# Idle places and shapes on TensorE in a decoder kernel's local attention: fillers, spreads and transposes moved or cut in halves

## The reference

```python
def attn_layer(x, Wqkv, qs, ksc, Wo):
    q, k, v = split(x @ Wqkv)                   # 16 heads of 64
    q, k = l2norm(q) * qs, l2norm(k) * ksc
    q = q * cos * scale + rotate_half(q) * sin * scale
    k = k * cos / scale + rotate_half(k) * sin / scale
    sim = q @ k (this window of 32 and the one before) * 8, masked
    out = softmax(sim) @ v
    return out @ Wo
def ffn_layer(x, g, bln, W1, b1, W2, b2):
    xn = (x - mu) / jnp.sqrt(var + 1e-05) * g + bln
    a, gate = jnp.split(xn @ W1 + b1, 2, -1)
    return a * gelu(gate) @ W2 + b2
for i in range(6):
    x = attn_layer(shift_tokens(x), ...) + x
    x = ffn_layer(shift_tokens(x), ...) + x
```

## Time and profile before

| | us |
|---|---|
| median of 3 runs | 1740.59 (1736.71 to 1741.67) |
| the profiled execution | 1734.79 |
| its span | 1732.9 |
| PE busy | 1564.7 |
| DVE busy | 1155.8 |
| ACT busy | 928.1 |
| POOL busy | 589.0 |

### The profile page before, as it was taken

The page is one execution under the profiler, slowest core; times in us unless marked ns, Lnnn a source line. Parts: engine busy times, 40 slices in busy tenths (PEclk is TensorE's granted clock), DMA queues, the critical chain, the costliest instruction groups (busy, mean ns, idle before and its releaser), DMA issues.

```text
span 1732.9 us, 37924 instructions
## 1 busy us (share of the span) xinstructions
PE 1564.7 (90%) x15445; PEld 857.0 (49%) x15445; DVE 1155.8 (67%) x2006; ACT 928.1 (54%) x1626; POOL 589.0 (34%) x552
## 2 busy tenths in 40 slices
PE   7887659999999998779899999999999999999996
PEld 2645335655555654223536455453635445463543
DVE  6686576666656564336767777776777777677773
ACT  2435333434443444336566667666766766676673
POOL 5462000000000000103655656554564645456461
PEclk9998679999999999879999999999999999999999
DMA  7134100000000000202131413313241331314120
GB/s 252 32 114 200 49 0 7 2 21 2 21 22 1 22 2 1 94 1 87 46 126 68 132 70 100 117 41 123 70 132 58 112 112 47 120 62 144 54 79 13
DMA packets 50666, 119.39 MB, mean 69 GB/s; under 512 B 15296, under 2 KB 20160, under 8 KB 48320
## 3 DMA queue, kind: packets, MB, share of 16 engines
q1 hardware_dynamic: 50496, 116.99, 20.4%
HBM read 37.52 MB, written 0.52 MB: 22 GB/s over the span
## 4 chain that ended last, share of the span: by engine, by line
PE 61%; DVE 19%; ACT 10%; issue 4%; DMA 3%; POOL 2%; SPq 1%; DVEq 0%; ACTq 0%; POOLq 0%
PE ps L415 5%; PE ps L425 5%; PE ps L398 4%; PE ps L1587 3%; PE ps L285 3%; PE ps L290 3%; PE ps L384 3%; PE ps L1640 3%; PE ps L274 3%; DVE nm L658 3%; PE ps L1649 2%; DMA big<-big 2%; ACT big L542 2%; DVE big L610 2%; DVE big L609 2%
## 5 line engine op out<-in xcount | busy, mean ns | idle before, releaser
L709 POOL TENSOR_TENSOR big<-big 128x512 f32<-128x512 f32 x112 | 142.6, 1273 | 307.9 <-DMA big<-big 307.2
L718 POOL TENSOR_TENSOR big<-big,nm 128x384 f32<-128x384 f32 x224 | 185.1, 847 | 164.7 <-DVE nm L651 164.7
L609 DVE TENSOR_TENSOR big<-ps,big 128x512 f32<-128x512 f32 x224 | 153.4, 685 | 85.6 <-ACT sq L487 55.9
L1431 POOL MEMSET big<- 128x512 f32 x1 | 0.5, 525 | 488.8 <-DVE x L1914 488.8
L542 ACT ACTIVATE big<-big 128x384 f32<-128x384 f32 x224 | 109.0, 522 | 92.4 <-DVE big L661 91.7
L610 DVE TENSOR_TENSOR big<-ps,big 128x512 f32<-128x512 f32 x224 | 152.1, 679 | 0.0
L415 PE MATMUL ps<-big 128*64 128x64 f32 x3584 | 129.9, 225 | 22.2 <-ACT big L554 21.4
L415 PEld LDWEIGHTS ps<-big 128*64 128x64 f32 x3584 | 115.7, 138 | 62.5 <-ACT big L554 42.5
L710 POOL TENSOR_TENSOR big<-big 128x512 f32<-128x512 f32 x112 | 144.3, 1288 | 0.0
L1874 DVE TENSOR_TENSOR big<-ps,fix 128x512 f32<-128x512 f32 x192 | 119.1, 682 | 37.2 <-PE ps L1587 36.8
L658 DVE TENSOR_REDUCE nm<-ps 128x4 f32<-128x384 f32 x224 | 112.4, 543 | 39.5 <-PE ps L384 37.5
(11 more groups left out here) (304 smaller groups left out, 2930.9 us busy)
## 6 DMA issues: line engine op xcount, KB each, us to landing
big<-big SPq DMA_DIRECT2D x224, 256.0 KB, 2.4
big<-big SPq DMA_DIRECT2D x112, 128.0 KB, 2.4
big<-in_F_w SPq DMA_DIRECT2D x6, 1536.0 KB, 6.7
big<-in_zero SPq DMA_DIRECT2D x8, 1088.0 KB, 12.6
big<-big SPq DMA_DIRECT2D x84, 64.0 KB, 2.0
big<-in_D_w SPq DMA_DIRECT2D x12, 256.0 KB, 3.1
big<-in_F_wo SPq DMA_DIRECT2D x6, 512.0 KB, 4.3
big<-in_F_w SPq DMA_DIRECT2D x6, 341.0 KB, 3.2
```

What stands on the lines that cost most here:

```text
L609: dve.tensor_tensor(tmp[:, i, w, :], ps[:, k, :], tb[:, 2 * w, :], ALU.mult).then_inc(*part.mark((key, b, p, 0)))
L718: pool.tensor_tensor(v, v, nm[:, p % 3, 16 + 4 * h:20 + 4 * h].unsqueeze(2).to_broadcast([128, 4, KW]), ALU.mult)\
```

## The change

- The transposes (`a_turn_pe`): 8 of 128 x 128 a step become 16 of 64 rows, alternating between the two halves of the array's rows; half c_ writes to bank 4 + c_. The values read the other layout.
- The spreads of a step stand between mask and scores, except those of pairs 1 to 3 that follow their k norm in steps 0 and 1.
- The head of a unit: V's product 5 ahead of the spreads of pair 0, down parts 0 and 1 behind them, down part 2 behind the scores of step 0.
- The up product's part 2 goes to bank 2 instead of 7.
- DVE's addition of the feed-forward moves from ahead of step 0 to behind the first reciprocal.
- The tail: the next unit's q product 0 ahead of the values of pair 6, k product 0 behind them, output product 6 behind q and k products 1.

```diff
@@ -274,20 +274,26 @@
...
-def a_qk_pe(pe, key, b, p):
-    kq, kk = p % 2, 2 + p % 2
+def a_q_pe(pe, key, b, p):
     if p == 0:
...
     if p < 2:
-        take(pe, kq)
+        take(pe, p)
     else:
         pe.wait_ge(*q_part.at((key, b, p - 2, 1)))
-    pe.matmul(ps[:, kq, :], Wqkv[:, 0, 128 * p:128 * p + 128], src_of(key, b), start=True, stop=True).then_inc(*full[kq].mark((key, b, "q", p)))
+    pe.matmul(ps[:, p % 2, :], Wqkv[:, 0, 128 * p:128 * p + 128], src_of(key, b), start=True, stop=True).then_inc(*full[p % 2].mark((key, b, "q", p)))
+
+def a_k_pe(pe, key, b, p):
+    kk = 2 + p % 2
     if p < 2:
...
     pe.matmul(ps[:, kk, :], Wqkv[:, 1, 128 * p:128 * p + 128], src_of(key, b), start=True, stop=True).then_inc(*full[kk].mark((key, b, "k", p)))
+
+def a_qk_pe(pe, key, b, p):
+    a_q_pe(pe, key, b, p)
+    a_k_pe(pe, key, b, p)
@@ -311,14 +317,13 @@
...
         a_ss_pe(pe, key, b, NP // 2 - 1)
-        a_v_pe(pe, key, b, 4)
+    a_v_pe(pe, key, b, 4)
+    a_v_pe(pe, key, b, 5)
+    if l2:
+        a_spread_q_pe(pe, key, b, 0)
+        a_spread_k_pe(pe, key, b, 0)
         if "down" in hooks:
             hooks["down"]()
-        a_spread_q_pe(pe, key, b, 0)
-        a_spread_k_pe(pe, key, b, 0)
-    else:
-        a_v_pe(pe, key, b, 4)
-    a_v_pe(pe, key, b, 5)
@@ -389,14 +394,19 @@
...
         pe.wait_ge(*scaled.at((key, b, p, h)))
-        if p == 0:
-            take(pe, 4 + h)
-        else:
-            pe.wait_ge(*turned.at((key, b, p - 1, h)))
         for j in range(4):
             at0 = 160 * j - (WIN if j % 2 else 0)
-            last = pe.transpose(ps[:, 4 + h, 128 * j:128 * j + 128], P[:, 2 * (p % 2) + h, at0:at0 + 128], ident[:, :])
-        last.then_inc(*full[4 + h].mark((key, b, "t", p)))
+            for c_ in range(2):
+                if h == 0 and j == 0:
+                    if p == 0:
+                        take(pe, 4 + c_)
+                    else:
+                        pe.wait_ge(*turned.at((key, b, p - 1, c_)))
+                rows = slice(64 * c_, 64 * c_ + 64)
+                last = pe.transpose(ps[:, 4 + c_, 256 * h + 64 * j:256 * h + 64 * j + 64], P[rows, 2 * (p % 2) + h, at0:at0 + 128],
+                                    ident[rows, rows], tile_position=(64 * c_, 0))
+                if (h, j) == (1, 3):
+                    last.then_inc(*full[4 + c_].mark((key, b, "t", p)))
@@ -413,7 +423,7 @@
...
                 last = pe.matmul(ps[64 * h:64 * h + 64, 6, 64 * m:64 * m + 64], vv[:, m // 2, 128 * p + 64 * h:128 * p + 64 * h + 64],
-                                 PT[:, 2 * (p % 2) + h, 128 * j + 64 * c_:128 * j + 64 * c_ + 64], start=True, stop=True,
+                                 PT[:, 2 * (p % 2) + c_, 256 * h + 64 * j:256 * h + 64 * j + 64], start=True, stop=True,
                                  tile_position=(0, 64 * h))
@@ -429,17 +439,20 @@
...
         a_mask_pe(pe, key, b, p, l2)
+        if l2 and p >= 2 and p + 2 < NP:
+            a_spread_k_pe(pe, key, b, p + 2)
+        if l2 and 0 < p < NP - 1:
+            a_spread_q_pe(pe, key, b, p + 1)
         a_scores_pe(pe, key, b, p, l2)
-        if l2 and p + 1 < NP:
-            a_spread_q_pe(pe, key, b, p + 1)
         if l2 and p == 0:
+            a_spread_q_pe(pe, key, b, 1)
             a_spread_k_pe(pe, key, b, 1)
+        if p in late:
+            late[p]()
         if p < 2:
             a_v_pe(pe, key, b, NT + 2 + p)
-        if l2 and p + 2 < NP:
-            a_spread_k_pe(pe, key, b, p + 2)
-        if p in late:
-            late[p]()
+            if l2:
+                a_spread_k_pe(pe, key, b, p + 2)
         if p >= 2:
@@ -448,16 +461,18 @@
...
 def a_tail_pe(pe, key, b, l2, nxt):
+    if nxt:
+        a_q_pe(pe, *nxt, 0)
     a_values_pe(pe, key, b, NP - 2)
+    if nxt:
+        a_k_pe(pe, *nxt, 0)
     a_out_pe(pe, key, b, NP - 3)
-    if nxt:
-        a_qk_pe(pe, *nxt, 0)
     a_turn_pe(pe, key, b, NP - 1)
-    a_out_pe(pe, key, b, NP - 2)
     if nxt:
...
             a_v_pe(pe, *nxt, v_with(l2, 1))
+    a_out_pe(pe, key, b, NP - 2)
     a_values_pe(pe, key, b, NP - 1)
@@ -677,8 +692,6 @@
...
             a_parts_dve(dve, key, b)
-        if "down" in early:
-            early["down"]()
         for p in range(NP):
@@ -2033,6 +2046,8 @@
...
+UP = (7, 7, 2)
+
 def f_up_pe(pe, l, b, i):
@@ -2040,15 +2055,18 @@
...
     pe.matmul(ps[0:m, 6, :], W1[:, DI + c0:DI + c0 + m], fxn, start=True, stop=True).then_inc(*full[6].mark(("F", l, b, "gate", i)))
-    take(pe, 7)
-    pe.matmul(ps[0:m, 7, :], W1[:, c0:c0 + m], fxn, start=True, stop=True).then_inc(*full[7].mark(("F", l, b, "up", i)))
-
-def f_down_pe(pe, l, b):
-    take(pe, Y)
-    for i, (c0, m) in enumerate(DIC):
+    take(pe, UP[i])
+    pe.matmul(ps[0:m, UP[i], :], W1[:, c0:c0 + m], fxn, start=True, stop=True).then_inc(*full[UP[i]].mark(("F", l, b, "up", i)))
+
+def f_down_pe(pe, l, b, parts):
+    for i in parts:
+        if i == 0:
+            take(pe, Y)
+        m = DIC[i][1]
         pe.wait_ge(*f_mul.at((l, b, i)))
         last = pe.matmul(ps[:, Y, :], W2[0:m, i, :], fh[0:m, i, :], start=i == 0, stop=i == 2)
-    last.then_inc(*full[Y].mark(("F", l, b, "f2")))
+    if i == 2:
+        last.then_inc(*full[Y].mark(("F", l, b, "f2")))
@@ -2059,7 +2077,7 @@
...
     return ({3: lambda: f_centre_pe(pe, *u), 4: lambda: f_var_pe(pe, *u), 6: lambda: f_up_pe(pe, *u, 0), 7: lambda: f_up_pe(pe, *u, 1),
-             "up": lambda: f_up_pe(pe, *u, 2), "down": lambda: f_down_pe(pe, *u)}, {})
+             "up": lambda: f_up_pe(pe, *u, 2), "down": lambda: f_down_pe(pe, *u, (0, 1))}, {0: lambda: f_down_pe(pe, *u, (2,))})
@@ -2072,7 +2090,7 @@
...
         f_up_pe(pe, *u, i)
-    f_down_pe(pe, *u)
+    f_down_pe(pe, *u, range(3))
@@ -2174,10 +2192,10 @@
...
     m = DIC[i][1]
-    dve.wait_ge(*full[7].at(("F", l, b, "up", i)))
+    dve.wait_ge(*full[UP[i]].at(("F", l, b, "up", i)))
     dve.wait_ge(*gg.at((l, b, i)))
-    dve.scalar_tensor_tensor(fh[0:m, i, :], ps[0:m, 7, :], b1[0:m, i:i + 1], fg[i % 2][0:m, :], ALU.add, ALU.mult).then_inc(*f_mul.mark((l, b, i)))
-    read(dve, 7, f_mul, (l, b, i))
+    dve.scalar_tensor_tensor(fh[0:m, i, :], ps[0:m, UP[i], :], b1[0:m, i:i + 1], fg[i % 2][0:m, :], ALU.add, ALU.mult).then_inc(*f_mul.mark((l, b, i)))
+    read(dve, UP[i], f_mul, (l, b, i))
@@ -2201,8 +2219,8 @@
...
     if u is not None:
-        early = {4: lambda: f_scale_dve(dve, *u), 6: lambda: f_mul_dve(dve, *u, 0), 7: multiply,
-                 "down": lambda: f_add_dve(dve, *u)}
+        early = {4: lambda: f_scale_dve(dve, *u), 6: lambda: f_mul_dve(dve, *u, 0), 7: multiply}
+        late[0] = lambda: f_add_dve(dve, *u)
     else:
...
     late[NP + 2] = lambda: f_shift_dve(dve, l, b)
```

## The result

The changed kernel takes 1754.29 us (median, 1750.92 to 1754.69); the kernel before, beside it on the same chip, 1741.13 (1736.71 to 1742.92). The ratio is 1.0071 with a 95% interval of [1.0055, 1.0086]: slower by 0.7%, where 1722 was forecast. The profiled execution took 1750.92 us, and its span is 16.2 us longer than before. Each profiled execution is among the faster ones of its kernel (1750.92 here, 1734.79 before), so 16.2 holds for these two, while the medians differ by 13.2.

A forecast was written before the change was run, and what follows sets the result against it. PE was taken to bind in full steps, a DVE, ACT and POOL chain at a unit's first steps and tail. Gains 11 x 0.95 = 10.4, 6.0 (bank) and 2.0 (first stage) sum to 18.4 us: median 1722, range 1709 to 1742.

The forecast's parts named there:

- nothing holds the gain up: End of a unit: output copy and the next unit's DVE ropes come 1.2 us earlier, so the gain of 0.95 a unit stays.
- the term for D0: Centre product to a unit's first DVE reduction: 1.0 us earlier a unit plus 6.0 for up 2's bank, 16.0 over ten units.
- The term of the bank: Up product's part 2, moved to bank 2, no longer waits for DVE to free bank 7 in six units: 6.0 us gained.
- The term of the tail itself: Last first reduction to next centre product: 1.15 us shorter a unit, with q product 0 filling PE's 1.13 wait before values 6.
- PE idles 0.6 there, hidden in nothing: Unit's head, around spreads of pair 0, two down parts and first scores: PE idle for 0.6 us.
- The bound by POOL (4.12): Full steps: PE's second half of the transposes follows POOL's scalings, so a step takes 4.12 us, not 4.00.
- the 0.93 lost at D1: Unit's second DVE reduction comes 0.93 us later than before; 0.7 comes back by the eighth reduction, net 0.2 lost.
- D0 to D1: Unit's first to second DVE reduction: 6.2 us instead of 4.3, by later exp(0) and the moved addition.
- Rivals 1 and 2: Transposes by halves take 0.86 us a step (1741 us, no change, chance 0.13); or 1.71 without overlap (1815, slower, 0.06).
- rival 3: Step 0 isn't delayed as worked out, as DVE can catch up: 0.8 us a unit more gained, 1713 us; chance 0.16.
- rival 4: Nothing of the tail remains, as POOL's ropes hold the next projection: about 9 us less gained, 1731 us; chance 0.12.
- by other ways: Whole kernel: a small loss by ways other than the named rivals; chance 0.03.

## Why the prediction was wrong

Between the first and the eleventh centre product the forecast and the trace are 26.7 us apart. By its steps:

1. **The tail's "nothing holds the gain up" failed** and with it most of the term for D0. The prediction followed the ropes to DVE and ACT, not to the transfers and POOL behind them. Earlier transfers start POOL's addition beside the shift copy. D0's sum is 277.0; at the most regular unit's 26.64 it would be 266.4, as predicted (266.1). So 10.6 us are lost here. With GpSimd's wait 7.2 of them come back, one stretch of low clock in the fourth unit's projection among them; the rest stays, most of it in the units that load Wo. The term of the bank comes back in another place there: PE's waits in the changed kernel have this line (L2059 is the up product):

```profile
PE ps L2059 <- DVEq L136: 6.3, 5, 2.1
```

Part 2 waits for no bank, as predicted, but in each of the five units that load Wo part 1 waits 0.58 to 2.15 us for DVE to free bank 7. The term of the tail itself was -1.15 a unit, measured -0.89, 2.6 too much in ten.

2. **The clock was left out.** Of the late turn 0 the prediction said that D1 comes later, not that PE, idle for 2.2 us in three waits, would in most units be given the lower clock behind it. D1 to D7 is 253.3; without low stretches (24.68, ten times) it is 246.8: 6.5 us. The step "PE idles 0.6 there, hidden in nothing" looked at the smaller gap.

3. **Full steps and steps 1 to 3 were mis-sized**, 5.0 us. The halves were right: 0.64 to 0.68 for a turn against 0.60, in place of 0.93. The bound by POOL (4.12) was not there: PE waits for nothing in the full step above. What the prediction counted as two changes of shape of 0.10 is 0.11 behind the turn, and 0.16 for the spreads between mask and scores. So 4.21. Alone, the halves give -0.18 and the spreads +0.16 a step: one pays for the other. Of the 0.93 lost at D1 only 0.2 to 0.3 came back, not 0.7.

4. **D0 to D1** was predicted as 6.2 and is 6.36; its working held, as late exp 1.26 (1.24 by the prediction) and addition 0.84 (0.69) show. The weak point is what the sum made of it: 1.9 lost at D1 for 1.0 gained at D0 was seen, and accepted because the tail and the full steps seemed to pay.

5. **Outside the ten units** lie the remaining 7.9 us. The first stage came out smaller than forecast: the first product behind it starts at 149.43 instead of 150.41, so 1.0 instead of 2.0 is gained there. The stages from there to the first centre product, which the change does not touch, last 730.7 instead of 728.5 in the two profiled executions, and why is open. The eleventh unit is 2.3 longer instead of 0.95 shorter, and what follows it 1.4 longer.

Of the rivals, none had this. The small loss "by other ways" had 0.03. Rivals 1 and 2 are wrong by the turn's 0.64, rival 3 by the first step's 6.36, and rival 4, nothing of the tail remains, was nearest in kind: not POOL's ropes held the projection, but the copy that met them. The stop of PE at the load of Wqkv spoils the halves when they stand alone (4.9 us in D3 to D4 of five units); in the changed kernel the profile has no such stop. Why it is absent there was not tried.

## What to carry to other kernels

A transfer or an engine that is made earlier lands beside new neighbours: follow it until something else waits, and look for an operation of DVE's that lasts 0.42 us alone and 1.4 beside GpSimd. A wait on PE costs more than its length if the lower clock comes behind it; here six cheap passes put into such a wait saved 3.9 us between two points, and the whole kernel's median fell from 1745.7 to 1733.04, for more reasons than the clock. When parts of a change are measured alone, keep what they need with them: tail and halves looked worthless one by one, and with GpSimd's wait, up 2's bank and a load in parts they give 1716.55 us, 1.3% under the kernel before.

## What the runs showed of the hardware

- A copy of 64 x 512 fp32 within SBUF on DVE takes 0.42 us. If an addition of GpSimd's (1.27) is under way when it starts, it ends 0.28 to 0.29 behind that addition, so it lasts 0.5 to 1.5; if it starts first, it keeps its 0.42, and the addition lasts up to 1.49.
- Sixteen transposes with 64 rows by 128 columns of weights and 64 moving columns, in turn on both row halves, take 0.64 us from start to start with a change of shape in it, where eight whole ones take 0.93.
- In the ten units of all these profiles the low clock stood for 3.4 us each time, or for 6.8. The changed kernel has it in some units and not in others with the same order of work, and filling a wait of 1.24 took it from 7 places to 3, so PE's waits make it likelier and do not decide it alone.
- PE can stop for 0.2 to 1.5 us in the middle of a row of passes, while 1.5 MB of weights are loaded in one transfer (7.0 us), because a 16 KB block of its program comes late: the stops of over 0.5 us end 1.2 to 1.6 behind the end of the block's transfer. In six parts of 256 KB, spread over some 20 us, the load leaves PE alone.
